# Wavelet mixing kernel: six weight buffers, the left-over line first, and minus identity in 32x32 tiles

## The reference

```python
yl, yh = _dwt2(x, 4)
yl_out = jnp.einsum('bixy,ioxy->boxy', yl, w_yl)
yh_out = yh[:-1] + [jnp.einsum('bicxy,iocxy->bocxy', yh[-1], w_yh)]
return _idwt2(yl_out, yh_out)
```

## Time and profile before

| | |
|---|---|
| median of 3 runs | 2045.24 us (2045.2 to 2045.88) |
| profiled execution, its own time | 2047.34 us |
| its span, first to last instruction | 2045.2 us |
| mean granted PE clock | 0.989 |
| busy share of the span | PE 91%, PEld 46%, DVE 41%, ACT 23% |
| moved by DMA | 827.16 MB, mean 404 GB/s |

### The profile page before, as it was taken

One profiled execution on the slowest core, in us unless ns is written; L12 is line 12 of the kernel. 1 busy time (PEld: TensorE's weight loads), 2 busy tenths in 40 slices (PEclk: granted clock), 3 DMA queues, 4 the chain that ended last, 5 costly groups with the idle time before them and its releaser, 6 DMA issues.

```text
span 2045.2 us, 44244 instructions
## 1 busy us (share of the span) xinstructions
PE 1853.3 (91%) x17580; PEld 945.5 (46%) x17580; DVE 837.0 (41%) x947; ACT 460.4 (23%) x1043; POOL 3.6 (0%) x7
## 2 busy tenths in 40 slices
PE   6999999999999679999998898898899889889886
PEld 3656666666666444444343333343333333334332
DVE  1222222222222454555444444444444444444443
ACT  1223222222322452121121121121121121112110
POOL 0000000000000000000000000000000000000000
PEclk9999999999999799999999999999999999999998
DMA  9999999999999695999999999999999999999998
GB/s 401 385 374 415 421 422 422 421 422 422 422 421 419 251 334 213 375 418 427 427 427 427 427 426 427 427 427 427 426 423 415 421 414 420 413 415 421 416 419 347
DMA packets 114794, 827.16 MB, mean 404 GB/s; under 512 B 12752, under 2 KB 13520, under 8 KB 17488
## 3 DMA queue, kind: packets, MB, share of 16 engines
q1 hardware_dynamic: 114768, 826.78, 97.7%
HBM read 558.29 MB, written 268.44 MB: 404 GB/s over the span
## 4 chain that ended last, share of the span: by engine, by line
DMA 52%; PE 10%; SPq 3%; issue 2%; DVE 0%; ACT 0%; DVEq 0%
DMA out<-x_sb 49%; PE ps L486 6%; DMA both<-w_full 2%; PE ps L476 2%; SPq L277 1%; PE ps L442 1%; SPq L282 1%; DMA x_sb<-x 1%; PE ps L437 1%; DMA both<-w_rest 0%; PE ps L466 0%; SPq L276 0%; DVE x_sb L720 0%; ACT both L610 0%; ACT both L570 0%
## 5 line engine op out<-in xcount | busy, mean ns | idle before, releaser
L486 PE MATMUL ps<-spread,const 128*128 128x512 f32 x2048 | 932.8, 598 | 109.5 <-DVE x_sb L720 109.5
L720 DVE TENSOR_TENSOR x_sb<-ps,x_sb 128x1024 f32<-128x1024 f32 x500 | 602.3, 1223 | 632.0 <-DMA x_sb<-x 403.0
L486 PEld LDWEIGHTS ps<-spread,const 128*128 128x128 f32 x2048 | 381.2, 190 | 645.2 <-issue 455.7
L624 ACT COPY spread<-ps 84x512 f32<-84x512 f32 x256 | 149.0, 582 | 938.5 <-PE ps L476 938.2
L350 PE MATMUL ps<-x_sb,const 32*32 32x512 f32 x8192 | 290.2, 601 | 36.6 <-DMA x_sb<-x 31.8
L363 PEld LDWEIGHTS ps<-const,work 128*128 128x128 f32 x2048 | 248.4, 194 | 56.4 <-ACT work L524 41.9
L476 PE MATMUL ps<-const,pick 128*84 128x512 f32 x512 | 261.3, 592 | 0.7 <-issue 0.7
L363 PE MATMUL ps<-const,work 128*128 128x84 f32 x2048 | 257.2, 278 | 2.9 <-ACT work L524 2.9
L524 ACT COPY work<-ps 128x512 f32<-128x512 f32 x256 | 131.4, 599 | 414.4 <-PE ps L350 414.4
L669 DVE COPY work<-ps 128x336 f32<-128x336 f32 x256 | 130.1, 508 | 176.3 <-PE ps L363 176.3
L350 PEld LDWEIGHTS ps<-x_sb,const 32*32 32x32 f32 x8192 | 138.3, 103 | 138.1 <-issue 98.7
(11 more groups left out here) (22 smaller groups left out, 218.9 us busy)
## 6 DMA issues: line engine op xcount, KB each, us to landing
x_sb<-x SPq DMA_DIRECT2D x498, 1024.0 KB, 13.3
out<-x_sb SPq DMA_DIRECT2D x250, 1024.0 KB, 16.8
both<-w_full SPq DMA_DIRECT2D x30, 896.0 KB, 6.6
work<-x SPq DMA_DIRECT2D x6, 1024.0 KB, 9.2
out<-work SPq DMA_DIRECT2D x6, 1024.0 KB, 10.8
both<-w_rest SPq DMA_DIRECT2D x6, 224.0 KB, 3.2
const<-consts SPq DMA_DIRECT2D x1, 888.0 KB, 4.5
```

Source lines behind the costliest of these rows:

```text
L486: last = nc.tensor.matmul(ps[:, 2 + k], const[:, SH + P * k:SH + P * k + P], spread[:, p], start=True, stop=True)
L624: nc.scalar.copy(spread[0:ROWS, p], ps[0:ROWS, p]).then_inc(s_copied[p], 1)
L720: nc.vector.tensor_tensor(part, ps[:, 2 + 2 * half:4 + 2 * half], part, ALU.add).then_inc(added[half], 1)
```

## The change: what it does

- **Buffers.** `work` and `both` become one buffer `work`. Six weight buffers (`w_sb`, one for each piece of a step) take the place of three; a weight load waits for the piece six earlier. The six early images lie where the analysis was and over weight buffers. Two of them are loaded at the end of the analysis, four between the last weight loads' places, each after a piece is mixed. `delta` and `stage` move within `work`, `spread` shares memory with the new `now`, and the staging of the first batch uses the front of `const`.
- **Left-over line.** It becomes step 0. Its 84 columns over four column groups are two pieces (14 and 7 columns each, `REST`), its weights one transfer of 1344 KB (`w_left`), and it is mixed before the full steps (`mix_left`).
- **Minus identity.** For full steps it is no longer taken of `diag`, but of `now`, a DVE copy of half a step (`copy_now`, 128 x 1344 elements), by `take_away`: four calls of 12 matmuls for each half step, of 112 columns in tiles of 32x32, over three banks. Each of the six pieces has a bank of its own. The calls stand between the halves of the pieces. The PE loop over full steps now holds eight calls of `take_away`, six pieces, and the turn back of the first batch's previous step (`first_coefs`).
- **Layout.** `mix_sb` has the batch innermost, so `build_low`, `build_high` and `copy_now` read runs of 112 or more elements; `copy_m` writes, and `copy_stage` reads, with a step of 8 elements.
- **Program form.** The mixing of ACT and DVE and the weight loads of SP are written out instead of looped; PE keeps its loop.

```diff
-WBUFS = 3
+GROUP3 = PARTS // 2
+REST = (U, U // 2)
+REST_BANK = 4
...
-        mix_sb = sb("mix_sb", [P, STEPS, BATCH, 4, ROWS])
+        mix_sb = sb("mix_sb", [P, STEPS, 4, ROWS, BATCH])
+        now = sb("now", [P, 4, GROUP3 * U, BATCH])
...
+        RING = 2 * IMAGE + CHANNELS * ROWS
+        DIAG = RING + PARTS * W_CHUNK
+        WORK = DIAG + 2 * 4 * U * QB
+        work = sb("work", [P, WORK])
+        w_sb = work[:, RING:DIAG].rearrange("p (a n) -> p a n", a=PARTS)
+        early = [0, IMAGE] + [RING + IMAGE * e for e in range(EARLY - 2)]
...
+            def load_w(p):
+                sp.dma_start(w_sb[:, p % PARTS], w_full[p]).then_inc(w_loaded[p % PARTS], 16)
...
+            sp.dma_start(w_left, w_left_in).then_inc(left_loaded, 16)
+            for p in range(4):
+                load_w(p)
+            sp.wait_ge(t_done, TURNS * SLOTS)
+            load_early(0)
+            sp.wait_ge(c_done, TURNS * HALVES)
+            load_early(1)
+            for p in range(4, PARTS * FULL):
+                if p < PARTS:
+                    pieces_mixed(1)
+                else:
+                    pieces_mixed(p - PARTS + 2)
+                load_w(p)
+            for e in range(2, EARLY):
+                pieces_mixed(PARTS * (FULL - 1) + e - 1 + 2)
                 load_early(e)
...
-            def mix(c, v, n):
-                for l in range(n):
-                    nc.tensor.matmul(ps[32 * l:32 * l + 32, a, 0:U * QB], const[:, NEG:NEG + CHANNELS],
-                                     diag[:, a, l].rearrange("p u n -> p (u n)"), start=True, stop=False)
+            def take_away(g, i, n):
+                if i == 0:
+                    pe.wait_ge(now_copied, (n + 4) // 4 if type(n) is int else n)
+                else:
+                    pe.wait_ge(neg_done, n)
+                pe.sem_inc(neg_begun, 1)
+                for j in range(GROUP3):
+                    c, q = GROUP3 * g + j, (i + j) % Q
+                    part = slice(32 * q, 32 * q + 32)
+                    for l in range(4):
+                        to = ps[32 * l:32 * l + 32, c, 0:U * QB].rearrange("p (u q b) -> p q u b", q=Q, b=BATCH)
+                        last = nc.tensor.matmul(to[:, q], const[part, NEG:NEG + CHANNELS],
+                                                now[part, l, U * j:U * j + U], start=i == 0, stop=False)
+                last.then_inc(neg_done, 1)
...
+            take_away(0, 0, 0)
+            take_away(0, 1, 1)
+            mix_left(0)
+            take_away(0, 2, 2)
+            mix_left(1)
+            take_away(0, 3, 3)
             with pe.Fori(0, FULL) as v:
-                for c in range(PARTS):
-                    mix(c, v, 4)
-            for c in range(PARTS):
-                mix(c, FULL, lines(FULL))
+                n = 8 * v + 4
+                mix(0, v, early_half)
+                pe.wait_ge(mixed_copied, 4 + PARTS * v)
+                pe.wait_ge(left_copied, 4)
+                take_away(1, 0, 2 * v + 2)
+                mix(0, v, late_half)
+                take_away(1, 1, n + 1)
+                mix(1, v, early_half)
+                take_away(1, 2, n + 2)
+                mix(1, v, late_half)
+                take_away(1, 3, n + 3)
+                mix(2, v, early_half)
+                mix(2, v, late_half)
+                first_coefs(v)
+                mix(3, v, early_half)
+                pe.wait_ge(mixed_copied, 4 + PARTS * v + GROUP3)
+                take_away(0, 0, 2 * v + 3)
+                mix(3, v, late_half)
+                take_away(0, 1, n + 5)
+                mix(4, v, early_half)
+                take_away(0, 2, n + 6)
+                mix(4, v, late_half)
+                take_away(0, 3, n + 7)
+                mix(5, v, early_half)
+                mix(5, v, late_half)
...
+            def copy_now(n):
+                if n:
+                    dve.wait_ge(neg_done, 4 * n)
+                at = GROUP3 * U * (n % 2)
+                nc.vector.tensor_copy(now[:], mix_sb[:, n // 2 + 1, :, at:at + GROUP3 * U]).then_inc(now_copied, 1)
...
+            for j in range(4, 2 + PARTS * FULL):
+                v, c = divmod(j - 2, PARTS)
+                if c == 1:
+                    copy_now(2 * v + 1)
+                if c == 4 and v + 1 < FULL:
+                    copy_now(2 * v + 2)
+                build_low(j)
```

More of the change, by code:

```diff
@@ L158, in wavelet_mix_kernel @@
         third = work[:, at:at + GROUP * ROWS]
[L159 to L168, removed]
@@ new lines, in mix_left @@
+            def mix_left(j):
+                u_all = REST[j]
+                pe.wait_ge(low_built[j], 1)
+                pe.wait_ge(high_built[j], 1)
+                for l in range(4):
+                    nc.tensor.matmul(ps[32 * l:32 * l + 32, REST_BANK + j, 0:u_all * QB], const[:, NEG:NEG + CHANNELS],
+                                     diag_of(j)[:, l].rearrange("p u n -> p (u n)"), start=True, stop=False)
+                pe.wait_ge(left_loaded, 16)
+                for u in range(u_all):
+                    for l in range(4):
+                        last = nc.tensor.matmul(ps[32 * l:32 * l + 32, REST_BANK + j, QB * u:QB * u + QB],
+                                                w_left[:, 4 * REST[0] * j + u_all * l + u], diag[:, j, l, u],
+                                                start=False, stop=u == u_all - 1)
+                last.then_inc(mixed[j], 1)
@@ new lines, in mix @@
+            def mix(c, v, columns):
+                a = c % 2
+                w = w_sb[:, c].rearrange("p (u l o) -> p u l o", u=U, l=4)
+                if columns.start == 0:
+                    pe.wait_ge(low_built[a], PARTS // 2 * v + c // 2 + 2)
+                    pe.wait_ge(high_built[a], PARTS // 2 * v + c // 2 + 2)
+                    pe.wait_ge(w_loaded[c], 16 * v + 16)
+                for u in columns:
+                    for l in range(4):
+                        last = nc.tensor.matmul(ps[32 * l:32 * l + 32, c, QB * u:QB * u + QB],
+                                                w[:, u, l], diag[:, a, l, u], start=False, stop=u == U - 1)
+                if columns.stop == U:
+                    last.then_inc(mixed[a], 1)
@@ new lines, in first_coefs @@
+            def first_coefs(v):
+                pe.wait_ge(first_staged, v + 1)
+                pe.wait_ge(d_copied, v + 1)
+                for q in range(Q):
+                    last = nc.tensor.matmul(ps[0:ROWS, 6, P * q:P * q + P], first_stage[:, ROWS * q:ROWS * (q + 1)],
+                                            const[:, EYE:EYE + P], start=True, stop=True, is_transpose=True)
+                last.then_inc(d_done, 1)
+            early_half, late_half = range(0, U // 2), range(U // 2, U)
@@ L465, in coefs_stage @@
+            for c in range(GROUP3):
+                nc.tensor.matmul(ps[:, c, 0:BATCH], const[:, EYE:EYE + P], const[:, EYE:EYE + BATCH], start=False, stop=True)
+            first_coefs(FULL)
+            def coefs_stage(v, k):
+                pe.wait_ge(staged, STEPS * (k - 1) + v + 1)
+                pe.wait_ge(d_copied, STEPS * k + v)
                 for q in range(Q):
@@ L499, in turn2 @@
                         coefs_stage(2 * (c - 1) + 1, batch)
-            for v in range(STEPS):
-                coefs_stage(v, 0, first=True)
-            pe.wait_ge(cleared, 3)
+            pe.wait_ge(cleared, 2)
+            pe.wait_ge(now_copied, 2 * FULL + 1)
             spread_stage(0, 0)
@@ L560, in _ @@
                 copy_m(v, BATCH - 1)
[L563 to L571, removed]
@@ L584, in _, with build_high @@
[L584 to L596, removed]
+            def build_high(j):
+                a, part = j % 2, slice(32 * (Q - 1), 32 * Q)
+                if j >= 2:
+                    act.wait_ge(mixed[a], j // 2)
+                nc.scalar.copy(diag_of(j)[part, :, :, BATCH * (Q - 1):BATCH * Q], lines_of(j)[part]).then_inc(high_built[a], 1)
@@ new lines, in copy_mixed, with copy_left @@
+            def copy_mixed(j):
+                act.wait_ge(mixed[j % 2], j // 2 + 1)
+                v, c = divmod(j - 2, PARTS)
+                nc.scalar.copy(mix_sb[:, v + 1, :, U * c:U * c + U],
+                               ps[:, c, 0:U * QB].rearrange("p (u q b) -> p q u b", q=Q, b=BATCH),
+                               ).then_inc(mixed_copied, 1)
+            def copy_left(j, l):
+                act.wait_ge(mixed[j], 1)
+                to, of = left_of(j, l)
+                nc.scalar.copy(to, of).then_inc(mixed_copied, 1)
@@ new lines, in _ @@
+            act.wait_ge(diag_cleared, 1)
+            act.wait_ge(m_copied, STEPS * (BATCH - 1) + 1)
+            build_high(0)
+            build_high(1)
+            for j in range(2):
+                for l in range(2):
+                    copy_left(j, l)
+                if j == 0:
+                    act.wait_ge(m_copied, STEPS * BATCH)
+                build_high(j + 2)
+            copy_first(0)
+            for j in range(2, 2 + PARTS * FULL):
```

(21 more changed lines are left out.)

191 lines of the change are left out of this document (92 added, 99 removed).

## The result

The changed kernel takes 2122.82 us (median of 4 runs, 2120.05 to 2125.0) against 2045.43 us before: ratio 1.0366, 95% interval 1.0339 to 1.0392, slower. The forecast was 2031.5, the range 2017 to 2056. What came is the rival R2, which had 0.18. The time lies in the lower half of what R2 was given (2108 to 2157, middle 2133).

A forecast was written before the change was run, and what follows sets the result against it. Transfers bound the synthesis, so time cut from the mixing shortens the whole: mixing ends at 762 instead of 773.4 (11.4 us), plus 2.4 us behind it, together 13.8 us, giving 2031.5 us; range 2017 to 2056.

The forecast's parts named there:

- R2: Rival, chance 0.18: every mixing pass refetches all PE instruction blocks, 31 or 43 us each; 2108 to 2157 us.
- PE's longer program: Mixing's first pass: three more instruction blocks at 5.37 us each, so it ends at 716 instead of 699.2.
- The sum: Mixing: first pass ends at 716, four unstalled passes of 11.5 us end at 762; 13.8 us gained with the tail.
- R1: Rival, chance 0.22: PE's mixing loop refetches one block a pass, 20 us more in all; 2051.5 us.
- the 5.37 us: First mixing pass: mean interval between PE's instruction stalls in the earlier trace, taken as the time per block.
- up to 3 us once: ACT's `copy_m` in the analysis, writing with a step: nothing, or this much extra once at the last batch.
- Builds and `copy_now`: DVE's work in a mixing pass: 18 builds and two `copy_now`, 12.3 to 12.9 us, just under DMA's 13.0.
- Six buffers: Mixing's weight loads run together: 2.16 us of DMA a piece instead of 2.57, 13.0 us a pass.
- Minus identity in small tiles: Mixing on PE: removes 5.8 us a pass and adds eight calls of 0.35 us, 2.8 a pass.

The follow-up runs named there:

- e1: Changed kernel with 11 small unused matmuls (44 PE instructions) ahead of the mixing; 2031.01 us, ratio 0.9903 to the kernel before.
- e4: Kernel before with 208 idle PE instructions at the end of each mixing-loop pass and 104 ahead of the loop; 2057.86 us.
- e6: Kernel of e1 with each weight load waiting for the piece three earlier instead of six; 2050.20 us, ratio 1.0011 to the kernel before.
- e7: Changed kernel with full-width minus identity of `diag` again, without `take_away` and `copy_now`; 2027.45 us, ratio 0.9893.
- e5: Kernel before with 208 idle PE instructions at the end of each mixing-loop pass and 64 ahead of the loop; 2121.22 us.
- e3: Kernel before with 208 idle PE instructions at the end of each mixing-loop pass, none ahead of the loop; 2087.99 us.
- e2: Changed kernel with 22 small unused matmuls (88 PE instructions) ahead of the mixing; 2061.98 us.

## Why the prediction was wrong

**The step that failed** is the one in "PE's longer program" and "The sum" that lets passes 2 to 5 run from memory: "716 + 46 = 762". The rival R1 had asked the right question, whether a ninth block fits, and the prediction gave "no" a chance of 0.40 in R1 and R2. The answer is that it doesn't: with the loop on at most seven blocks (e1, e4, e6, e7) no pass was refetched, with eight and the way back 106 or 203 into the eighth (e5, the changed kernel) every later pass was, and the four passes took 132.8 us where 46 were given. By the Trainium skill, Runtime: NRT & Kernel Launch, section Instruction fetch mechanics, PE's memory is first in, first out and has 2048 instructions in blocks of 256. The trace agrees: nine transfers a pass, which is every block of eight and the one ahead. R1's form, one refetched block a pass, appeared in no run.

**Size of R2.** 32 to 34 us a pass against 12 in e1, where 31 to 43 was given. From the end of the first pass to the end of the loop the changed kernel takes 848.6 - 715.8 = 132.8 us, e1 762.5 - 715.0 = 47.5; the 85.3 between them are nearly all of the 88.7 between the two spans (2118.3 and 2029.6).

**The rest, read in e1**, where the loop lies on seven blocks and nothing else is changed:

- Sum: 2031.4 predicted for the span, 2029.6 measured; 2031.5 for the median, 2031.01 measured. The first synthesis matmul: "about 765", measured 765.73.
- That is luck in good part. The mixing was to start at 672 and the first pass to end at 716. The start was at 679.15 and the end at 715.0: seven late at the start, and the blocks came faster than the 5.37 us taken from the earlier trace rows. In the changed kernel they came 3.74 us apart, near the shortest of the earlier trace rows, 3.85. The term was mis-sized by a third. The DMA share was 0.57 in 674 to 716 there, against 0.83 in 674 to 699 of the earlier trace rows; that this made the blocks faster is not shown. The stage gained 19.8 us (111.9 to 92.1) and not 13.8, and the start, 6.5 us later than before (673.66 and 667.18), took the surplus away.
- The late start (transposes of the last batch at 673.66 in e1, 675.77 in the changed kernel, 667.18 before) arises in the first 160 us of the analysis. Its cause is open: `copy_m` costs 784 ns instead of 441, within the bound of 953, but that was priced at up to 3 us once, and the time between later batches is the same. A part of it is spread between executions. The transposes begin at 667.2 to 671.3 in the four traces with the analysis of before (the kernel before, e3, e4, e5) and at 670.9 to 680.3 in the six with the changed one. Up to some 60 us the granted clock of 20 to 40 us goes with it: 1.00 in the kernel before, e2 and e6, 0.83 in e3 to e5, 0.74 in the other four; the fifth transfer of PE's instructions begins at 54 to 55, 57 and 59 to 61 us. Runs of the kernel before on other chips also lay between 2044.3 and 2057.7.
- `take_away`: 0.39 us from its start to that of the records behind it, 0.35 taken. The row below is from e1. Pass: 11.8 (between rows of like place in passes 3 and 4, 727.53 and 739.29), 11.5 taken.

```profile
724.53 0.46 PE L477 MATMUL ps<-now,const 32*32 32x112 f32 x24
724.92 0.70 PE L506 MATMUL ps<-work 128*32 128x32 f32 x56
```

- Builds and `copy_now`: 1.3 to 1.6 us was given for `copy_now`, 0.539 for a build unless contiguous sources help. They do; groups of e1, 714 to 762:

```profile
L816 DVE COPY work<-mix_sb 32x448 f32<-32x448 f32 x69 | 26.4, 383 | 13.5 <-PE ps L506 12.8
L671 ACT COPY work<-mix_sb 32x448 f32<-32x448 f32 x23 | 12.9, 562 | 0.6
L829 DVE COPY now<-mix_sb 128x1344 f32<-128x1344 f32 x7 | 6.0, 860 | 1.2 <-PE ps L477 1.0
```

 DVE has 6 x 3 x 0.383 + 2 x 0.86 = 8.6 us of work a pass, not 12.3. It would not have become the bound.
- Six buffers: the mechanism was right, and by e6 nothing of the gain in the kernel's time is left without them.
- Minus identity in small tiles: 5.8 us a pass were to be saved and 2.8 spent. Against e7 the pass is shorter by 0.1 us. The records of the full-width form overlap those of the mixing: 0.96 was its duration, and from its start to that of the weights' records it is 0.75 (719.36 to 720.11 above). The small tiles' 16 matmuls a piece took the loop from 1462 to 1769 instructions, and so to an eighth block.
- A slip in the sum: 716 and 39 us of DMA are 755, not 757. Nothing rests on it, as PE was last.

## What to carry to other kernels

A loop's price includes where its instructions lie. Count all instructions of an engine in a loop, find the block borders from the stalls of its first pass, and see that the loop and the block ahead fit in what is held; a row of instruction transfers in later passes gives the failure away at once. Where they don't fit, padding ahead of the loop can cure it, but fewer instructions are the lasting cure. And the duration of a pipelined matmul group is not what its removal saves: take the distance between the starts of its neighbours.

## What was not expected of the hardware

- The loss is not one stall at the way back but all blocks, and not at every way back from an eighth block: 0 of 4 lost on seven blocks, 1 of 4 at 35 instructions into the eighth, 2 of 4 at 42, 4 of 4 at 106 and 203.
- A move by 44 instructions, which do nothing, changed a kernel of 2.1 ms by 4%.
- The granted clock was 0.50 to 0.55 in the refetched passes of the changed kernel, with PE busy 52 to 60% of the time, and 0.53 in the written-out loop, against 0.97 in e1. In the refetched passes of e5 it was 0.75 to 0.84, with PE busy 58 to 61%, and they were no shorter.
